# Layer 1's loop entry: ScalarE's tiles and copies placed before a norm, and GpSimd's power placed after both splits

## The chip, the cores and the metric

The kernel runs on one core of one Trainium2 chip. The metric is the device time of one execution in microseconds, the median of several runs; lower is better.

## What is computed

Four graph layers are applied one after the other to x of shape (32, 256, 128), each with a residual sum and a layer norm:

```python
x = layernorm(x + L0(x, adj))   # graph convolution with two batch norms
x = layernorm(x + L1(x, src, dst, adj))   # attention over 256 edges
x = layernorm(x + L2(x, adj))   # three matrix products with adj * adj
x = layernorm(x + L3(x, adj))   # dense graph attention
```

Layer 0 ends with a batch norm over all batches, so no batch can start layer 1 before all have finished layer 0. Layer 1 gathers the rows of its input x1 at the two ends of each edge and projects them with two matrices:

```python
Xq = H @ W_lin.T;  Xv = H @ W_val.T
e = sum(leaky_relu(Xq[src] + Xq[dst]) * a) + log(adj[src, dst] + eps)
attn = segment_softmax(e, src)
Y = segment_sum(attn * Xv[dst], src);  return Y @ W_out.T
```

The change lies where the norm after layer 0 is made and layer 1's gather and projection are done.

## The kernel before

The 32 batches are worked on in pairs. A pair is a *slot*, s = 0 or 1, and two slots make a *step* p = 0 to 7 (IT = 8); q = 2p + s counts the slots. Each engine has a program of its own, written out by hand in the order in which it works, and they meet at semaphores. Instructions on one engine run in that order: one that waits holds all behind it.

In this stage one step goes through these pieces:

- `bn_out_slot(p, s)` on ScalarE (line 1551) applies the batch norm to one slot of layer 0's output and writes the tile bnt.
- `turn_out_slot(p, s)` on TensorE (line 1963) transposes that tile into PSUM bank s.
- `sum0_slot(p, s)` on VectorE (line 875) adds it to x (tile xin, loaded by SP after an earlier sum has gone) and writes the sum to xn, which is part of keep_x.
- `variance0(p)` on VectorE (lines 190 to 203) takes mean and variance of both slots, and waits until the norm of the step before has been applied. It ends with ln_v.
- `ln_power(p)` on GpSimd (lines 209 and 212) takes the power -0.5 of ln_v, and then ln_b, mean times that power.
- `apply0(p)` on VectorE (line 905) normalizes slot 0, and `scale0(p)` on ScalarE (line 1543) slot 1. Both wait for ln_b.
- `split_x1(p, s)` on GpSimd (lines 581 and 583) splits the normalized slot into a high part (a cast) and a low part (a difference). It waits for the norm of that slot, and for the gather that used this buffer one step earlier.
- `gather_slot(p, s)` on TensorE (line 1982) multiplies the parts with the 0/1 edge matrices: 8 matmuls of 128x512 a slot, into two PSUM banks. It waits for the split and, since project uses the same banks, for both projected copies of the same slot one step earlier.
- `gathered_slot(p, s)` on ScalarE (line 1523) copies the result to SBUF; `project(p)` on TensorE (lines 1993 and 1997) projects it; `projected(p, s)` on ScalarE (lines 1533 and 1535) copies out z and vall.
- `leaky_slot` on VectorE (line 885) and `score_slot` on TensorE (line 2006, 16 matmuls of 4 columns a step) make the edge scores.

What sets the order around the change: TensorE's loop for p = 2, 3, 4 is gather(p), turn_out(p + 3), score(p - 1), project(p). ScalarE's program comes to it with edge_log and scale0(3), and then loops:

```python
scale0(3)
with act.Fori(2, IT - 3) as p:
    for s in range(2):
        bn_out_slot(p + 3, s, False)
        gathered_slot(p, s)
    scale0(p + 2)
    for s in range(2):
        projected(p, s)
```

VectorE's loop body for p is variance0(p + 2), leaky(p - 1), sum0(p + 3), apply0(p + 2). GpSimd ends its own entry with ln_power(3) and then loops over p = 3 to 6: split_x1(p, 0), ln_power(p + 1), split_x1(p, 1). `act.Fori` and `pool.Fori` are loops that the engine itself runs, with registers and a branch. After the loops steps 5 to 7 are finished without new tiles, and layers 2 and 3 follow, with layer 1's end woven into layer 2's start.

Of the kernel before, what the change touches and what calls it, by code (L numbers as in the profile page):

```python
# [34 lines left out]
IT = Q // 2  # L35
# [8 lines left out]
def build(nc, x, adj, adj_t, w1_t, w2_t, bn_cols, wv_t, wq_t, a_head, wo_t, src,  # L44
          dst, edge_cols, l2w1, l2w2, l2w3, l3w, l3a, l3w_t, out):
    ctx = ExitStack()
    with ctx:
# [11 lines left out]
        def bank(k, n=1):  # L59
            return psum[:, k:k + n, :]  # L60

        def gathered_bank(s):

            return bank(2 + 2 * s, 2)
# [86 lines left out]
        def wait_apart(eng, own, signal, value):  # L151


            if not isinstance(value, int):
                value = eng.snap(value)
            eng.wait_ge(own, 1)
            eng.wait_ge(signal, value)
# [48 lines left out]
        def ln_power(pool, p, ln):  # L206

            pool.wait_ge(ln.var, p + 1 - ln.late)
            pool.tensor_tensor(ln.r[:].rearrange("p s k -> p (s k)"), ln.v[:].rearrange("p s k -> p (s k)"), mhalf[:],  # L209
                               ALU.pow).then_inc(ln.root, 1)  # L210
            pool.wait_ge(ln.root, p + 1 - ln.late)
            pool.tensor_tensor(ln.b[:].rearrange("p s k -> p (s k)"), ln.m[:].rearrange("p s k -> p (s k)"),  # L212
                               ln.r[:].rearrange("p s k -> p (s k)"), ALU.mult).then_inc(ln.rstd, 1)
# [112 lines left out]
        def row(p):  # L326

            return lambda s, t, j: xn[:, 2 * p + s, t, j, :]
# [146 lines left out]
        def _(pool):  # L475
# [97 lines left out]
            def split_x1(p, s, first):  # L573

                q = 2 * p + s
                pool.wait_ge(ln0_done[s], q + 1)
                if not first:

                    pool.wait_ge(g_done, q - 1)
                    pool.wait_ge(x1_lo, q)  # L580
                pool.tensor_copy(x1s[0][:, s], xn[:, q]).then_inc(x1_hi, 1)
                wait_apart(pool, pz, x1_hi, q + 1)
                pool.tensor_tensor(x1s[1][:, s], xn[:, q], x1s[0][:, s], ALU.subtract).then_inc(x1_lo, 1)
# [7 lines left out]
                split_x1(2, s, False)  # L591
            ln_power(pool, 3, ln0)
            with pool.Fori(3, IT - 1) as p:
                split_x1(p, 0, False)
                ln_power(pool, p + 1, ln0)
                split_x1(p, 1, False)
            for s in range(2):
                split_x1(IT - 1, s, False)

# [838 lines left out]
        def _(act):  # L1438
# [82 lines left out]
            def gathered_slot(p, s):  # L1521
                act.wait_ge(g_done, 2 * p + s + 1)
                act.activation(g1[:, s].rearrange("p j k e -> p j (k e)"), gathered_bank(s), ACT.Copy).then_inc(g_out, 1)
# [5 lines left out]
            def projected(p, s):  # L1529
                q = 2 * p + s  # L1530

                act.wait_ge(z_done, q + 1)
                act.activation(z1[:, s, :], bank(2 + 2 * s)[:, 0, :], ACT.Copy).then_inc(z_ready, 1)
                act.wait_ge(ve_done, q + 1)
                act.activation(vall[:, :, bass.ds(2 * q, 2), :],
                               bank(3 + 2 * s)[:, 0, :].rearrange("p (t j d) -> p t j d", t=ET, j=2), ACT.Copy).then_inc(ve_out, 1)

            def scale0(p):

                act.wait_ge(ln0.rstd, p + 1 - ln0.late)  # L1540
                for k in range(4):
                    y = row(p)(1, k // 2, k % 2)
                    i = act.activation(y, y, ACT.Identity, bias=ln0.b[:, 1, k:k + 1], scale=ln0.r[:, 1, k:k + 1])  # L1543
                i.then_inc(ln0_done[1], 2)

            def bn_out_slot(p, s, first):
                q = 2 * p + s
                if not first:

                    act.wait_ge(t1_done, q - 1)  # L1550
                act.activation(bnt[:, s, :], oraw[:, q, :], ACT.Identity, bias=bco[:, 3, 2:3], scale=bco[:, 2, 2:3]).then_inc(bnt_ready, 1)
# [18 lines left out]
            def edge_log():  # L1570

                act.wait_ge(a_edge_done, 1)
                act.activation(log_a[:], bank(6)[:, 0, 0:E], ACT.Ln, bias=log_eps[:]).then_inc(log_ready, 1)
# [39 lines left out]
            for s in range(2):  # L1613
                bn_out_slot(4, s, False)
                projected(1, s)
            edge_log()
            scale0(3)
            with act.Fori(2, IT - 3) as p:
                for s in range(2):
                    bn_out_slot(p + 3, s, False)  # L1620
                    gathered_slot(p, s)
                scale0(p + 2)
                for s in range(2):
                    projected(p, s)
# [789 lines left out]
```

## Time and profile before

| | |
|---|---|
| three runs | 559.87, 561.19, 562.27 us; median 561.19 |
| span of the profiled execution | 558.5 us (first to last instruction; the page gives no other time of it) |
| TensorE busy | 533.0 us, 95% of the span |
| VectorE, ScalarE, GpSimd busy | 419.8, 371.9, 202.1 us |
| chain that ended last | TensorE 83%, VectorE 11%, ScalarE 2%, GpSimd 2% |

The span is one execution as the hardware profiler saw it; the runs are timed without it and take in what lies around the span. Times in the rows are microseconds from the first instruction. PE is TensorE, ACT ScalarE, DVE VectorE, POOL GpSimd. The granted clock is given as a share of TensorE's 2.4 GHz. Starts of matmuls are measured and their ends modelled, so neighbouring ones overlap in the rows.

### The profile page before, as it was taken

What the parts mean: (1) busy time and instruction counts of PE and PEld (TensorE: products, weight loads), DVE (VectorE), ACT (ScalarE), POOL (GpSimd) and SP (SyncE); (2) the same over time, 40 slices, a digit from 0 to 9 for tenths busy, and PEclk for the clock granted to TensorE, in tenths of its full rate; (3) what the DMA queues carried; (4) which work ended last, traced back from release to release, by engine and by line L of the source; (5) the groups of instructions that cost most, each with busy time, mean ns of one, the idle gap of its engine ahead of it and who ended that gap; (6) DMA issues with size and microseconds to landing.
All of it is one profiled execution on the core that took longest, in us unless ns stands there. A gap on an engine that the chain in (4) does not pass through costs nothing.

```text
span 558.5 us, 11129 instructions
## 1 busy us (share of the span) xinstructions
PE 533.0 (95%) x3522; PEld 467.1 (84%) x3522; DVE 419.8 (75%) x1465; ACT 371.9 (67%) x752; POOL 202.1 (36%) x245
## 2 busy tenths in 40 slices
PE   7999998988999989999999999999999999999974
PEld 6998534676888988998989999999998998989953
DVE  5899577997595643589787687788778676788797
ACT  4775793755756536355785785786688677676773
POOL 4960442254567303216127126216215214310203
PEclk9999999996999999999999999999999999999997
DMA  6621000222100000000000100100100100100002
GB/s 188 195 84 38 0 0 18 71 78 62 38 0 1 2 1 1 1 1 2 1 1 2 39 0 1 38 0 0 38 0 0 38 1 0 38 2 0 21 20 76
DMA packets 28418, 15.29 MB, mean 27 GB/s; under 512 B 2352, under 2 KB 28080, under 8 KB 28384
## 3 DMA queue, kind: packets, MB, share of 16 engines
q1 hardware_dynamic: 27536, 13.38, 8.3%
q0 software_dynamic: 560, 1.25, 0.8%
q8 instruction: 15, 0.25, 0.2%
q10 hardware_dynamic: 288, 0.26, 0.1%
q14 instruction: 19, 0.16, 0.1%
HBM read 10.69 MB, written 4.19 MB: 27 GB/s over the span
## 4 chain that ended last, share of the span: by engine, by line
PE 83%; DVE 11%; ACT 2%; issue 2%; POOL 2%; POOLq 0%; DVEq 0%; ACTq 0%
PE psum L293 15%; PE psum L295 15%; PE psum L294 15%; PE psum L2135 10%; PE psum L1934 5%; PE psum L1982 3%; PE psum L2077 3%; PE psum L2087 3%; PE psum L2006 2%; PE psum L1993 2%; PE psum L1997 2%; PE psum L2181 2%; PE psum L2163 2%; PE psum L1861 1%; DVE soft L1087 1%
## 5 line engine op out<-in xcount | busy, mean ns | idle before, releaser
L209 POOL TENSOR_TENSOR ln_r<-ln_v,mhalf 128x8 f32<-128x8 f32 x25 | 41.3, 1653 | 204.6 <-DVE ln_v L203 204.6
L2135 PE MATMUL psum<-l2w_s,h 128*128 128x128 f32 x512 | 59.7, 275 | 0.0
L2135 PEld LDWEIGHTS psum<-l2w_s,h 128*128 128x128 f32 x512 | 59.0, 192 | 0.6
L293 PE MATMUL psum<-qt_hi,l2w_s_hi 128*128 128x512 f32 x128 | 52.8, 412 | 0.0
L295 PE MATMUL psum<-qt_hi,l2w_s_lo 128*128 128x512 f32 x128 | 50.7, 396 | 0.0
L294 PE MATMUL psum<-qt_lo,l2w_s_hi 128*128 128x512 f32 x128 | 50.6, 395 | 0.0
L287 ACT ACTIVATE keep_x<-keep_x,ln_b,ln_r (+1 forms) x104 | 42.7, 487 | 2.6 <-POOL ln_b L212 2.6
L1664 ACT ACTIVATE h<-psum 128x512 f32<-128x512 f32 x60 | 34.9, 594 | 11.7 <-PE psum L295 11.6
L293 PE MATMUL psum<-wgt_hi,h_hi 128*128 128x256 f32 x128 | 37.1, 290 | 0.9 <-DVE h_lo L1064 0.9
L295 PE MATMUL psum<-wgt_hi,h_lo 128*128 128x256 f32 x128 | 35.8, 280 | 0.0
L294 PE MATMUL psum<-wgt_lo,h_hi 128*128 128x256 f32 x128 | 35.7, 279 | 0.0
L1064 DVE SCALAR_TENSOR_TENSOR h_lo<-psum,h_hi 128x1024 fp32r<-128x1024 f32 x16 | 19.6, 1225 | 18.5 <-ACT h_hi L1655 18.5
L190 DVE BATCH_NORM_STATS2 ln_st<-keep_x 128x6 f32<-128x128 f32 (+1 forms) x152 | 31.1, 277 | 1.3 <-ACT keep_x L1543 0.8
L1087 DVE SCALAR_TENSOR_TENSOR soft<-keep_x,wa 128x128 f32<-128x128 f32 x96 | 29.6, 374 | 0.0
L1934 PE MATMUL psum<-hraw,w2t 128*128 (+1 forms) x64 | 29.3, 608 | 0.0
L1075 DVE TENSOR_TENSOR s_lo<-psum,s_hi 128x512 fp32r<-128x512 f32 x16 | 11.1, 691 | 24.1 <-ACT s_hi L1668 24.1
L1660 ACT ACTIVATE qt_hi<-psum 128x1024 fp32r<-128x1024 f32 x16 | 16.4, 1024 | 19.1 <-PE psum L295 19.1
L295 PEld LDWEIGHTS psum<-qt_hi,l2w_s_lo 128*128 128x128 f32 x128 | 24.1, 188 | 5.8
L1071 DVE TENSOR_TENSOR qt_lo<-psum,qt_hi 128x1024 fp32r<-128x1024 f32 x16 | 19.5, 1221 | 11.7 <-ACT qt_hi L1660 11.7
L294 PEld LDWEIGHTS psum<-qt_lo,l2w_s_hi 128*128 128x128 f32 x128 | 24.2, 189 | 4.4
L293 PEld LDWEIGHTS psum<-qt_hi,l2w_s_hi 128*128 128x128 f32 x128 | 24.1, 189 | 4.4
L1685 ACT ACTIVATE soft<-soft,zm 128x256 f32<-128x256 f32 x56 | 27.7, 498 | 0.0
(297 smaller groups left out, 1760.7 us busy)
## 6 DMA issues: line engine op xcount, KB each, us to landing
keep_x<-in_x SPq DMA_DIRECT2D x32, 128.0 KB, 2.8
xin<-in_x SPq DMA_DIRECT2D x32, 128.0 KB, 2.2
out_x<-ob SPq DMA_DIRECT2D x24, 128.0 KB, 1.8
out_x<-keep_x SPq DMA_DIRECT2D x8, 128.0 KB, 2.0
l2w_raw<-in_l2w POOLq DMA_DIRECT2D x1, 512.0 KB, 4.9
adjs<-in_adj_t ACTq DMA_DIRECT2D x2, 128.0 KB, 2.7
adjs<-in_adj SPq DMA_DIRECT2D x2, 128.0 KB, 3.0
l2w_s<-in_l2w POOLq DMA_DIRECT2D x1, 256.0 KB, 4.8
```

What stands on the lines that cost most here:

```text
L190: i = dve.bn_stats(ln.st[:, s, k, :], y(s, k // 2, k % 2))
L209: pool.tensor_tensor(ln.r[:].rearrange("p s k -> p (s k)"), ln.v[:].rearrange("p s k -> p (s k)"), mhalf[:], ALU.pow).then_inc(ln.root, 1)
L287: i = act.activation(y(s, k // 2, k % 2), y(s, k // 2, k % 2), ACT.Identity, bias=ln.b[:, s, k:k + 1], scale=ln.r[:, s, k:k + 1])
L293: pe.matmul(o, lhs[0], rhs[0], start=start, stop=False)
L294: pe.matmul(o, lhs[0], rhs[1], start=False, stop=False)
L295: return pe.matmul(o, lhs[1], rhs[0], start=False, stop=stop)
L1064: dve.scalar_tensor_tensor(out=h1[1][:, s].rearrange("p j t f -> p (j t f)"), in0=bank(2 * s, 2).rearrange("p k c -> p (k c)"), scalar=0.0 ...
L1087: i = dve.scalar_tensor_tensor(out=soft[:, s, k, c * D:(c + 1) * D], in0=xn[:, q, k // 2, k % 2, :], scalar=1.0, in1=wa[:, c, :], op0=ALU. ...
L1664: act.activation(h2[:, s, g, :], bank(4 + g)[:, 0, :], ACT.Relu).then_inc(h2_out, 1)
L1685: i = act.activation(soft[:, s, k, :], soft[:, s, k, :], ACT.Exp, bias=zm[:, 2, s, k:k + 1], accum_out=rs[:, s, k:k + 1])
L1934: i = pe.matmul(bank(s)[:, 0, :], w2t[:, k, :], hraw[:, k, q, :], start=(k == 0), stop=(k == 1))
L2135: i = pe.matmul(bank(s)[:, 0, k * D:(k + 1) * D], h2[:, s, g, j * N + t * P:j * N + (t + 1) * P], l2w3_s[:, g, :], start=(g == 0), stop=(g ...
```

## The change

On ScalarE the tiles of step 5 and the copies of gather(2), which were the first half of the loop's first turn, are put ahead of scale0(3); the loop is written out in Python (three turns, p = 2, 3, 4), and its later turns keep their order. On GpSimd both slots are split before ln_power, in each turn of the loop. No other engine's program is touched.

```diff
@@ GpSimd
             with pool.Fori(3, IT - 1) as p:
-                split_x1(p, 0, False)
+                for s in range(2):
+                    split_x1(p, s, False)
                 ln_power(pool, p + 1, ln0)
-                split_x1(p, 1, False)
             for s in range(2):
                 split_x1(IT - 1, s, False)
@@ ScalarE
             edge_log()
+            for s in range(2):
+                bn_out_slot(5, s, False)
+                gathered_slot(2, s)
             scale0(3)
-            with act.Fori(2, IT - 3) as p:
-                for s in range(2):
-                    bn_out_slot(p + 3, s, False)
-                    gathered_slot(p, s)
+            for p in range(2, IT - 3):
+                if p > 2:
+                    for s in range(2):
+                        bn_out_slot(p + 3, s, False)
+                        gathered_slot(p, s)
                 scale0(p + 2)
                 for s in range(2):
                     projected(p, s)
```

## Rows read from the trace of the kernel before

**Rows 1.** The page: busy time of TensorE, and its clock in 40 slices.

```profile
PE 533.0 (95%) x3522; PEld 467.1 (84%) x3522; DVE 419.8 (75%) x1465; ACT 371.9 (67%) x752; POOL 202.1 (36%) x245
...
PEclk9999999996999999999999999999999999999997
```

**Rows 2.** TensorE's timeline at the entry: start, duration, work, [idle before <- releaser].

```profile
123.71 0.40 PE L1982 MATMUL psum<-sel,x1s_lo 128*128 128x512 f32 x1
127.28 1.11 PE L1963 MATMUL psum<-ident,bnt 128*128 128x128 f32 x4 [3.17 <-ACT bnt L1551]
...
129.72 3.42 PE L2006 MATMUL psum<-head_a,l 128*128 128x4 f32 x16
```

**Rows 3.** Windows, TensorE alone: stretch, length, busy, granted clock, DMA share, GB/s.

```profile
124.11:127.28 3.17, 0.01 (x1) 0.95 0.56 165
127.28:130.50 3.22, 2.79 (x13) 0.50 0.00 1
...
137.20:140.50 3.30, 3.30 (x19) 1.00 0.00 0
```

**Rows 4.** ScalarE's timeline at the entry and the loop's first turn.

```profile
120.03 0.47 ACT L1573 ACTIVATE log_a<-psum,log_eps 128x256 f32<-128x256 f32 x1
124.80 1.65 ACT L1543 ACTIVATE keep_x<-keep_x,ln_b,ln_r 128x128 f32<-128x128 f32 x4 [4.30 <-POOL ln_b L212]
...
128.66 1.01 ACT L1523 ACTIVATE g<-psum 128x1024 f32<-128x1024 f32 x1
131.59 1.65 ACT L1543 ACTIVATE keep_x<-keep_x,ln_b,ln_r  x4 [1.92 <-POOL ln_b L212]
...
139.42 0.81 ACT L1551 ACTIVATE bnt<-keep_x,bco 128x512 f32 x1
```

**Rows 5.** VectorE's timeline: ln_v of step 4, and the leaky ops at 150 us.

```profile
129.24 0.17 DVE L203 TENSOR_SCALAR ln_v<-ln_ag 128x8 f32<-128x8 f32 x1
...
150.10 1.28 DVE L885 SCALAR_TENSOR_TENSOR l<-z 128x512 f32<-128x512 f32 x2
```

**Rows 6.** GpSimd's timeline: casts of the splits, and powers.

```profile
126.25 0.61 POOL L581 CAST x1s_hi<-keep_x 128x512 fp32r x1 [1.48 <-DVE keep_x L905]
...
129.49 1.65 POOL L209 TENSOR_TENSOR ln_r<-ln_v,mhalf 128x8 f32<-128x8 f32 x1 [1.20 <-DVE ln_v L203]
...
140.81 0.61 POOL L581 CAST x1s_hi<-keep_x 128x512 fp32r x1 [7.26 <-PE psum L1982]
...
142.83 1.64 POOL L209 TENSOR_TENSOR ln_r<-ln_v,mhalf 128x8 f32<-128x8 f32 x1
...
150.71 1.15 POOL L581 CAST x1s_hi<-keep_x 128x512 fp32r x1 [3.83 <-PE psum L1982]
...
172.50 0.70 POOL L581 CAST x1s_hi<-keep_x 128x512 fp32r<-128x512 f32 x1 [0.17 <-POOL x1s_lo L583]
```

**Rows 7.** TensorE's timeline in the loop: gather(3) first and last, (4), (5), (6).

```profile
138.54 0.48 PE L1982 MATMUL psum<-sel,x1s_hi 128*128 128x512 f32 x1
...
142.12 0.39 PE L1982 MATMUL psum<-sel,x1s_lo 128*128 128x512 f32 x1
...
148.43 0.48 PE L1982 MATMUL psum<-sel,x1s_hi 128*128 128x512 f32 x1
...
158.33 0.48 PE L1982 MATMUL psum<-sel,x1s_hi 128*128 128x512 f32 x1
...
167.81 0.47 PE L1982 MATMUL psum<-sel,x1s_hi 128*128 128x512 f32 x1
```

**Rows 8.** ScalarE's timeline: scale0(7), the last of its kind.

```profile
165.06 1.65 ACT L1543 ACTIVATE keep_x<-keep_x,ln_b,ln_r 128x128 f32<-128x128 f32 x4 [1.70 <-POOL ln_b L212]
```

**Rows 9.** TensorE's timeline near the end.

```profile
542.05 0.66 PE L2286 MATMUL psum<-ident,soft 128*128 128x128 f32 x4 [2.51 <-ACT soft L1769]
```

**Rows 10.** Windows near the end, TensorE alone.

```profile
546.00:547.00 1.00, 1.00 (x7) 0.61 0.02 8
```

**Rows 11.** TensorE's timeline at the start of layer 2.

```profile
199.68 0.38 PE L293 MATMUL psum<-l2w_s_hi,pt_hi 128*128 128x256 f32 x1 [1.60 <-ACT y1t L1591]
```

## The prediction

> **What bounds the kernel now.** I read the page first: TensorE is busy 95% of the span, and its granted clock is full in every slice but the one at 126 to 140 us [rows 1]. So what delays TensorE at that place comes out at the end one for one. Then TensorE's timeline there: after the last matmul of gather(2), at 123.71, nothing starts until turn_out(5) at 127.28, 3.17 us idle, and the next score takes 3.42 us [rows 2]. The windows show why that is long: the granted clock stands at 0.50, the 1.2 GHz level, from the restart on, and is back by 137.20 [rows 3]. The release named is ScalarE's bnt tile, and ScalarE's timeline shows what stood ahead of it: idle 4.30 us, waiting for GpSimd's ln_b before scale0(3) at 124.80 [rows 4]. The tile for step 5 is queued behind a norm that TensorE doesn't need yet.
>
> In the loop that follows TensorE is the bound: gather(p) starts at 138.54, 148.43, 158.33 and 167.81, that is every 9.89, 9.90 and 9.48 us, with no idle time in between [rows 7]. But a second chain runs nearly as long. gather(p) may not write its PSUM bank before projected(p-1, slot 0) has left it, which on ScalarE stands behind scale0(p+1), which waits for GpSimd's power(p+1), which stands behind split(p, slot 0), which waits for the first half of gather(p-1). Its length: gather to split 2.28 (148.43 to 150.71), split to power 2.02 (140.81 to 142.83) [rows 6, 7]; power to scale 2.10 (129.49 to 131.59) [rows 4, 6]; scale to next gather 2.75 (165.06 to 167.81) [rows 7, 8]. Together 9.15 us: a slack of 0.3 to 0.75 a step.
>
> **The change, part by part.**
>
> *ScalarE's entry.* Step 5's two tiles and the copies of gather(2) go ahead of scale0(3). ScalarE is free at 120.50 [rows 4], so the first tile (0.81) is ready at 121.3, long before TensorE wants it. The second copy waits for gather(2)'s end, 123.71 + 0.40 = 124.11 [rows 2], takes 1.01 [rows 4], and scale0(3) starts at 125.12, 0.32 late. Behind that wait stand scale0(3) and, on VectorE, the statistics of step 4, whose ln_v moves from 129.41 to 129.73 [rows 5]. On TensorE the wait of 3.17 goes, and the half-rate work behind it: from the last matmul of a gather to the next gather is 6.31 us in the loop (142.12 to 148.43) [rows 7], so TensorE is done with project(2) at 130.0.
>
> *What is late next.* gather(3) needs projected(2, slot 0), behind scale0(4), behind power(4). On GpSimd split(3, 0) starts at 126.25 as before [rows 6], because VectorE's half of the norm isn't moved. Now split(3, 1) comes next: 126.25 + 2.02, a hand-over of 0.17 (the row at 172.50, where two splits stand together), + 2.02 = 130.46, later than ln_v, so power(4) starts there instead of at 129.49 [rows 6]. Then 2.10 and 2.75: gather(3) starts at 135.31, against 138.54. The entry gives 3.23 us, not the whole of the stall and the slow clock, and TensorE idles 5.3 us (130.0 to 135.3).
>
> *The clock after that gap.* 3.17 idle us were enough to halve it [rows 2, 3], 1.60 were not [rows 1, 11]. So I take it as halved at 135.3. How long? Near the end TensorE starts again at 542.05 and the clock is back at 546.8 (0.61 mean in that microsecond), 4.7 us [rows 9, 10]; after the gap at 124 it took 9.9 (127.28 to 137.2) [rows 2, 3]. gather(3) is one dense run of wide matmuls as the work at 542 is, while that at 127 was transposes and 4-column scores; I take 4.7, a loss of 2.35. Bounds: none, and all of gather(3) at half, 3.97.
>
> *GpSimd's order in the loop.* Power(p+1) now comes after split(p, 1) too. That puts 0.17 + 2.02 into the chain above: 9.15 + 2.19 = 11.34 us, longer than TensorE's own 9.9. This is the price of the change, and it is paid in each of the three steps, since power(5), (6) and (7) all gate a gather. GpSimd has no queue behind the power that suffers; what waits is ScalarE's scale, and behind it both projected copies, then TensorE. What split(p, 1) gains by going earlier is worth nothing: gather(p, 1) was not waiting for it. In the step behind gather(4) the cast took 1.15 beside VectorE's leaky ops (from 150.10) instead of 0.61 [rows 5, 6]; hidden now, it would be on the chain, so I add 0.54 once, with 0 and twice that as bounds. The Trainium skill (SBUF — State Buffer, "two separate sides") has GpSimd and a VectorE op with two SBUF inputs exclude each other for a whole instruction, whichever starts first. The trace agrees; by that rule the cast goes free if it starts first, and the sum below is 0.54 less.
>
> *The loop written out, and DMAs.* At its turn ScalarE's bnt starts at 139.42 with no idle time ahead [rows 4], so unrolling removes nothing to be seen: 0. No DMA is moved. SP's loads of xin wait for VectorE's sums, which move with the tiles; they were not what anything here waited for, and the steps get longer, not shorter: 0.
>
> **The sum.** gather(3) 135.31, its end 135.31 + 3.97 + 2.35 = 141.63; split(4, 1) needs that end: + 0.17 + 2.02 + 2.10 + 2.75 = gather(4) at 148.67 (before 148.43). gather(5) at + 11.34 + 0.54 = 160.55 (158.33). gather(6) at + 11.34 = 171.89 (167.81). That is 4.1 us late, and from there the order is unchanged and TensorE bound, so it stays. The gaps of about 1.5 us a step are below the 1.60 that left the clock alone. Span 558.5 + 4.1 = 562.6. The page gives no time of that execution beyond its span; the median of the runs, 561.19, stands 2.7 above it for what lies around, so 565.3.
>
> **The rivals.**
>
> *The clock hardly falls.* Three chain steps from 135.31 without loss or lock: 169.33, 1.5 late, 562.7; with the lock 563.2. For it: two gaps with a low clock are all that this trace has, and their low stretches differ by a factor of two. Against: the gap is longer than the one that did halve the clock. 0.16.
>
> *The clock stays low as long as before.* All of gather(3) at half: end 143.25, gather(4) 150.29, gather(6) 173.51, 5.7 late, 566.9. 0.12.
>
> *The other side: the entry's gain is kept.* This needs power(p+1) to stay off the chain, that is, split(p, 1) to add less than the slack of 0.75. Then the steps stay at 9.89, 9.90, 9.48 and gather(6) starts at 164.58, 3.2 early, 558.0; with the 2.35 of slow clock 0.9 early, 560.3. For it: TensorE is the bound in every loop row today. Against: a split costs 2.02 wherever it stands. 0.17, of which 0.11 for the faster end.
>
> *The change doesn't do what it says.* If TensorE's gap at 124 isn't the queue on ScalarE, gather(3) stays at 138.54 and only the longer steps are left: 5.3 late, 566.5. Against it: the transposes start 0.13 us after the bnt tile is done. 0.05.
>
> **How the numbers follow.** The forecast has 0.50. About 0.5% (2.8 us: 558.4 to 564.0) is what a measurement here can tell from no change. Faster: 0.11 from the third rival. Same: the first rival (0.16), the rest of the third (0.06) and 0.04 of the forecast's low side, 0.26. Slower: 0.46 + 0.12 + 0.05 = 0.63. The range goes from the third rival's 560.3 to the long clock with one more lock, 567.5; outside are the 0.11 below and a little above.
>
> **What would show it.** Right: turn_out(5) follows gather(2) at once; a new TensorE gap of about 5 us ahead of gather(3), released by ScalarE's vall copy; then gaps of 1 to 2 us ahead of gather(4), (5) and (6), gathers some 11.3 us apart, power(p+1) directly behind the second split with ScalarE idle 3 to 4 us for ln_b in each step. A low clock at 134 to 141 shows the second term. Wrong: gathers still 9.9 apart, or no gap ahead of gather(3).

## The result and the profile after

The changed kernel takes 567.5 us (median of seven runs, 564.01 to 569.2) against 561.19 before: ratio 1.0102, interval 1.0081 to 1.0123. It is slower by about 1%. The seven runs lie in two groups, 564.0 to 565.8 us at a mean granted clock of 0.985 or 0.986 and 567.5 to 569.2 at 0.980 or 0.981; the profiled execution is of the second, and no trace shows which low stretch the first group lacks. The profiled execution took 567.63 us, its span 565.9, 7.4 above the span before.

The page after: busy time, and TensorE's clock in 40 slices; they answer to [rows 1].

```profile
PE 534.0 (94%) x3522; PEld 467.8 (83%) x3522; DVE 416.3 (74%) x1465; ACT 370.9 (66%) x752; POOL 200.9 (36%) x245
...
PEclk9999999997998999999999999999999999999987
```

TensorE has the same work and nearly the same busy time (534.0 us against 533.0); what is new is mostly waiting. There are two places with a low clock in layer 1 instead of one. TensorE's timeline after, the first matmul of gather(3), (4), (5), (6) and (7), to be held against [rows 7]:

```profile
135.44 0.77 PE L1986 MATMUL psum<-sel,x1s_hi 128*128 128x512 f32 x1 [5.18 <-ACT vall L1535]
...
148.75 0.47 PE L1986 MATMUL psum<-sel,x1s_hi 128*128 128x512 f32 x1 [0.75 <-ACT vall L1535]
...
160.48 0.47 PE L1986 MATMUL psum<-sel,x1s_hi 128*128 128x512 f32 x1 [1.59 <-ACT vall L1535]
...
172.31 0.47 PE L1986 MATMUL psum<-sel,x1s_hi 128*128 128x512 f32 x1 [2.36 <-ACT vall L1535]
...
183.35 0.48 PE L1986 MATMUL psum<-sel,x1s_hi 128*128 128x512 f32 x1
```

Four gaps, all released by ScalarE's vall copy, stand where [rows 7] had none. gather(3) is 3.1 us earlier than before, gather(4) 0.3 later, gather(5) 2.2 later, gather(6) 4.5 later. The queue behind it, on ScalarE, shows scale0(3) to scale0(7); they answer to [rows 4, 8]:

```profile
125.05 1.64 ACT L1543 ACTIVATE keep_x<-keep_x,ln_b,ln_r 128x128 f32<-128x128 f32 x4
...
132.69 1.65 ACT L1543 ACTIVATE keep_x<-keep_x,ln_b,ln_r 128x128 f32<-128x128 f32 x4 [6.00 <-POOL ln_b L212]
...
146.00 1.65 ACT L1543 ACTIVATE keep_x<-keep_x,ln_b,ln_r 128x128 f32<-128x128 f32 x4 [3.10 <-POOL ln_b L212]
...
157.73 1.65 ACT L1543 ACTIVATE keep_x<-keep_x,ln_b,ln_r 128x128 f32<-128x128 f32 x4 [3.94 <-POOL ln_b L212]
...
169.56 1.65 ACT L1543 ACTIVATE keep_x<-keep_x,ln_b,ln_r 128x128 f32<-128x128 f32 x4 [4.05 <-POOL ln_b L212]
```

scale0(3) no longer waits; each of the others waits 3 to 6 us for GpSimd. GpSimd's timeline after shows why; it answers to [rows 6] (casts of the turn p = 5, its power, the cast and the power of p = 6):

```profile
151.02 0.83 POOL L581 CAST x1s_hi<-keep_x 128x512 fp32r x1 [5.06 <-PE psum L1986]
...
153.79 0.61 POOL L581 CAST x1s_hi<-keep_x 128x512 fp32r x1 [0.25 <-POOL x1s_lo L583]
...
155.78 1.64 POOL L209 TENSOR_TENSOR ln_r<-ln_v,mhalf 128x8 f32<-128x8 f32 x1
...
162.75 0.61 POOL L581 CAST x1s_hi<-keep_x 128x512 fp32r x1 [5.06 <-PE psum L1986]
...
167.23 2.02 POOL L209 TENSOR_TENSOR ln_r<-ln_v,mhalf 128x8 f32<-128x8 f32 x1
```

The power starts 4.5 to 4.8 us after the first cast, where [rows 6] had 2.0 (140.81 to 142.83), and that with GpSimd idle 5 us before the cast: the engine isn't short of time, its order is wrong for the one who waits. The granted clock after, in windows with TensorE alone (stretch, length, busy, clock, DMA share, GB/s), answers to [rows 3]:

```profile
133.00:134.00 1.00, 0.00 (x0) 0.98 0.71 185
134.00:135.00 1.00, 0.00 (x0) 0.50 0.72 195
...
140.00:141.00 1.00, 1.00 (x5) 0.60 0.00 0
178.00:179.00 1.00, 1.00 (x3) 0.67 0.00 0
181.00:182.00 1.00, 1.00 (x5) 0.62 0.00 0
```

The slow clock after the old stall (127 to 137) is gone. There are two others: 134.0 to 140.8, over the gap and most of gather(3), and 178.3 to 181.8, over the first half of project(6). The latter makes gather(6) to gather(7) 11.04 us instead of 9.38, 1.66 more.

The 7.4 us of the span are therefore 4.5 at gather(6), 1.66 behind it, and the rest near the end: the transposes of [rows 9] start at 548.66 after, 6.6 late (0.45 of it picked up somewhere in 365 us), and from there to the end it is 17.24 us against 16.45, because the clock was already halved when they started.

```profile
548.66 1.11 PE L2290 MATMUL psum<-ident,soft 128*128 128x128 f32 x4 [2.52 <-ACT soft L1773]
```

They took 0.66 before. That last 0.8 goes with neither part of the change: of the kernels below, GpSimd's part alone has 0.66 there and so has the kernel with both fillers, while ScalarE's part alone and the kernel with one turn have 1.12. Each of these is one execution, so no edit can be made answerable for it.

### The profile page after: what moved, and what is told of

Read it like the earlier page. It is cut to its first block, busy times and chain, and to the rows that moved or that the text cites. A ratio compares the mean times of both kernels' runs of the same rounds, so it can differ in the third digit from the quotient of the medians.

```text
span 565.9 us, 11089 instructions
## 1 busy us (share of the span) xinstructions
PE 534.0 (94%) x3522; PEld 467.8 (83%) x3522; DVE 416.3 (74%) x1465; ACT 370.9 (66%) x752; POOL 200.9 (36%) x245
## 4 chain that ended last, share of the span: by engine, by line
PE 81%; DVE 9%; POOL 4%; ACT 4%; issue 1%; POOLq 0%; DVEq 0%
PE psum L293 15%; PE psum L295 15%; PE psum L294 15%; PE psum L2139 9%; PE psum L1938 5%; PE psum L1986 4%; PE psum L2081 3%; PE psum L2091 3%; PE psum L2185 2%; PE psum L2167 2%; PE psum L1865 1%; ACT keep_x L1543 1%; POOL x1s_lo L583 1%; POOL ln_r L209 1%; PE psum L2010 1%
## 5 line engine op out<-in xcount | busy, mean ns | idle before, releaser
L1668 ACT ACTIVATE h<-psum 128x512 f32<-128x512 f32 x60 | 34.8, 594 | 11.7 <-PE psum L295 11.6
L1986 PE MATMUL psum<-sel,x1s_hi 128*128 128x512 f32 x64 | 27.6, 432 | 11.1 <-ACT vall L1535 9.9
L1071 DVE TENSOR_TENSOR qt_lo<-psum,qt_hi 128x1024 fp32r<-128x1024 f32 x16 | 19.6, 1222 | 11.7 <-ACT qt_hi L1664 11.7
```

The source lines that it names most:

```text
L1668: act.activation(h2[:, s, g, :], bank(4 + g)[:, 0, :], ACT.Relu).then_inc(h2_out, 1)
L1986: i = pe.matmul(gathered_bank(s)[:, j, :], x1s[h][:, s, t, j, :], sel[:, t].rearrange("p k e -> p (k e)"), start=(n == 0), stop=(n == 3))
```

## The experiments

Nine kernels were run; each is compared with runs of the kernel before on the same chip.

### The two parts apart

ScalarE's part alone is the change without its GpSimd hunk. GpSimd's part alone:

```diff
             with pool.Fori(3, IT - 1) as p:
-                split_x1(p, 0, False)
+                for s in range(2):
+                    split_x1(p, s, False)
                 ln_power(pool, p + 1, ln0)
-                split_x1(p, 1, False)
```

Expected of ScalarE's part:

> The change's ScalarE part alone, GpSimd in its old order. Chain theory (the cost is GpSimd's second split ahead of the power, which gates each gather): power(4) starts at ln_v, about 129.8, so gather(3) starts near 134.6 instead of 135.4, after a TensorE gap of 4 to 5 us that still halves the clock for some microseconds; after it the gathers are 9.9 to 10 us apart again with no gap, gather(6) is 1 to 4 us ahead of the kernel before (167.81), and the time is 557 to 560.5 us. Rival (ScalarE's new queue order or its written-out loop costs the time): slower than before, near 565 to 567, with gaps ahead of gather(4) to gather(6) as in the changed kernel.

Expected of GpSimd's part:

> The change's GpSimd part alone, ScalarE as before. Chain theory: the stall at 124 and its slow clock stay, gather(3) stays near 138.5, and then the gathers are 11.3 to 11.9 us apart with TensorE gaps of 1 to 2.4 us released by ScalarE's vall copy; gather(6) near 173.1, time 566 to 568.5 us. Rival (the loss is the slow clock after the new 5 us gap, which this kernel does not have): gathers 9.9 us apart, time within 1 us of before.

Measured: ScalarE's part alone 558.79 us against 560.78, ratio 0.9962 (0.9943 to 0.9981), a gain of 0.4%. GpSimd's part alone 567.86 against the same, 1.0125 (1.0098 to 1.0152). TensorE's timeline, gather(3) to (6), first of ScalarE's part, then of GpSimd's:

```profile
134.52 0.76 PE L1986 MATMUL psum<-sel,x1s_hi 128*128 128x512 f32 x1 [3.83 <-ACT vall L1535]
...
147.19 0.48 PE L1986 MATMUL psum<-sel,x1s_hi 128*128 128x512 f32 x1
...
157.08 0.48 PE L1986 MATMUL psum<-sel,x1s_hi 128*128 128x512 f32 x1
...
166.53 0.47 PE L1986 MATMUL psum<-sel,x1s_hi 128*128 128x512 f32 x1
```

```profile
138.83 0.48 PE L1982 MATMUL psum<-sel,x1s_hi 128*128 128x512 f32 x1
...
150.24 0.47 PE L1982 MATMUL psum<-sel,x1s_hi 128*128 128x512 f32 x1 [1.26 <-ACT vall L1535]
...
162.08 0.47 PE L1982 MATMUL psum<-sel,x1s_hi 128*128 128x512 f32 x1 [1.72 <-ACT vall L1535]
...
173.91 0.47 PE L1982 MATMUL psum<-sel,x1s_hi 128*128 128x512 f32 x1 [2.35 <-ACT vall L1535]
```

With GpSimd's old order the gathers behind gather(4) are 9.89 and 9.45 apart and there is no gap after the first (gather(3) itself runs at the low clock, from 133.8 to 140.6); with its new order alone they are 11.41, 11.84 and 11.83 apart, though this kernel has the old stall and no 5 us gap behind it. Its gather(6) came at 173.91, 0.8 later than expected. The loss belongs to GpSimd's order; ScalarE's written-out loop costs nothing that shows.

### One turn only

The turn p = 4 alone splits both slots before the power; the other turns keep the order.

```diff
+            split_x1(3, 0, False)
+            ln_power(pool, 4, ln0)
+            split_x1(3, 1, False)
+            for s in range(2):
+                split_x1(4, s, False)
+            ln_power(pool, 5, ln0)
-            with pool.Fori(3, IT - 1) as p:
+            with pool.Fori(5, IT - 1) as p:
```

> The kernel before, with GpSimd's new order in one turn only (p = 4, so power(5) comes behind both splits and gates gather(4)). Chain theory: gather(3) to gather(4) takes 11.3 us instead of 9.89, the next two stay at 9.90 and 9.48, the time is 1.4 us above before. Rival (one turn's slack absorbs it): 9.9 in all three.

```profile
138.47 0.48 PE L1988 MATMUL psum<-sel,x1s_hi 128*128 128x512 f32 x1
...
149.75 0.47 PE L1988 MATMUL psum<-sel,x1s_hi 128*128 128x512 f32 x1 [1.12 <-ACT vall L1541]
...
159.64 0.48 PE L1988 MATMUL psum<-sel,x1s_hi 128*128 128x512 f32 x1
...
169.15 0.47 PE L1988 MATMUL psum<-sel,x1s_hi 128*128 128x512 f32 x1
```

TensorE's timeline again: 11.28, then 9.89 and 9.51. One turn costs its 1.4 us once and nothing else moves. The one timed run, 561.77 against 560.78, is 1.0 above, which alone would prove little.

### The slow clock

Useless matmuls fill the gaps; they write a bank that nobody reads at that time. The first filler, ahead of gather(3):

```diff
-            with pe.Fori(2, IT - 3) as p:
+            gather(2, False)
+            turn_out(5, False)
+            score(1)
+            project(2)
+            pe.wait_ge(log_ready, 1)
+            spin(10, 6)
+            with pe.Fori(3, IT - 3) as p:
```

> The changed kernel, with 10 useless 128x256 matmuls (about 4.7 us) put into TensorE's gap ahead of gather(3). They replace no work and write a bank that nobody reads. If the slow clock of gather(3) is a term of its own: clock 1.00 from 124 to 150, gather(3) lasts 3.97 us instead of 6.4, gather(4) starts near 146.8 instead of 148.75, and the gathers behind it stay 11.3 to 11.9 apart; the time falls by about 2 us against the changed kernel. If all of the loss were the clock: the gathers come back to 9.9 apart and the time to that before or below.

The second, ahead of gather(6):

```diff
             project(IT - 3)
+            pe.wait_ge(sm, 2)
+            spin(4, 6)
             gather(IT - 2, False)
```

> The changed kernel with 4 useless 128x256 matmuls (about 1.9 us) in the last of the new gaps, the 2.36 us ahead of gather(6); they replace no work and write a bank that nobody reads. If that gap is what lets the clock fall behind it (in the changed kernel at 178.3, well after TensorE had started again): clock 1.00 from 150 to 200, gather(6) unmoved near 172.3, gather(7) 9.4 us behind it at 181.7 instead of 183.35. If the 4-column scores at 176 to 178 make the fall by themselves: the slow stretch stays, and gather(7) with it.

And both:

> The changed kernel with both fillers (10 matmuls ahead of gather(3), 4 ahead of gather(6)). What is then left of the loss is the longer chain alone: clock 1.00 from 124 to 200, gather(3) to (6) 11.3 to 12 us apart, gather(7) 9.4 behind gather(6), near 180.3; so about 3.2 us above the kernel before, 564 us (563 to 565.5), and 2.5 to 3.5 us below the changed kernel. If the fillers only moved the waiting, the time stays near 567.

TensorE's timeline with both, gather(3) to (7):

```profile
135.00 0.47 PE L1986 MATMUL psum<-sel,x1s_hi 128*128 128x512 f32 x1 [0.89 <-ACT vall L1535]
...
147.00 0.47 PE L1986 MATMUL psum<-sel,x1s_hi 128*128 128x512 f32 x1 [1.85 <-ACT vall L1535]
...
158.73 0.47 PE L1986 MATMUL psum<-sel,x1s_hi 128*128 128x512 f32 x1 [1.59 <-ACT vall L1535]
...
170.58 0.47 PE L1986 MATMUL psum<-sel,x1s_hi 128*128 128x512 f32 x1 [0.63 <-ACT vall L1535]
...
179.95 0.48 PE L1986 MATMUL psum<-sel,x1s_hi 128*128 128x512 f32 x1
```

Both fillers give 563.7 us against 560.86, ratio 1.0058 (1.0037 to 1.008): what the longer chain costs alone, net of the entry's gain. The clock is 1.00 from 124 to 200, and gather(6) to (7) is 9.37. The gathers stay 11.7 to 12.0 apart, so the chain remains. Against the 1.0102 of the changed kernel, the low clock in layer 1 is some 2.5 us of the loss, an estimate from the two ratios. The first filler alone made gather(3) to (4) 11.99 (136.02 to 148.01) instead of 13.31; that is 1.3 us for the slow clock, not the 1.9 expected, since the chain there is some 0.6 longer than forecast: with gather(3) at full clock the cast of split(4, 0) meets VectorE's leaky ops and takes 1.08 us instead of 0.61, and the difference behind it 1.53 instead of 1.27. Its one time is 566.88, so the 2 us expected of it don't show: it kept a slow stretch ahead of and in gather(6), 171.2 to 174.6, and one near the end. The second alone (564.81 in one run) took the stretch at 178 away; the windows of that kernel:

```profile
175.00:180.00 5.00, 5.00 (x35) 1.00 0.00 0
180.00:185.00 5.00, 5.00 (x30) 1.00 0.00 0
```

gather(6) starts at 172.19 there and gather(7) at 181.57, as forecast. The three profiled kernels with this gap of 2.35 or 2.36 us open (the changed one, GpSimd's part alone, the first filler alone) all show a low stretch there, the two with it filled show none: it takes the gap, and the scores by themselves don't do it.

### The scale taken off TensorE's path

Here GpSimd keeps the new order, and ScalarE's projected copies, with the next tiles behind them, go ahead of the scale in the turns p = 2, 3, 4; the turn p = 5 stays as it was:

```diff
             for p in range(2, IT - 3):
                 if p > 2:
-                    for s in range(2):
-                        bn_out_slot(p + 3, s, False)
-                        gathered_slot(p, s)
-                scale0(p + 2)
+                    gathered(p)
                 for s in range(2):
                     projected(p, s)
+                for s in range(2):
+                    if p + 4 < IT:
+                        bn_out_slot(p + 4, s, False)
+                scale0(p + 2)
```

> The changed kernel, GpSimd's new order kept, with ScalarE's projected copies of a step (and the next tiles) put ahead of scale0(p + 2) in the turns p = 2, 3, 4, so that the scale, and the power behind it, no longer gate gather(3), (4) and (5). Chain theory (GpSimd's order costs only because the scale stands ahead of the projected copies): no gap ahead of gather(3), which starts near 130.0; no gap released by the vall copy ahead of gather(4) and (5); gather(6), whose turn keeps the old order, still about 11.3 us after gather(5). A new wait is likely ahead of score(2), because VectorE makes leaky(2) behind the statistics that wait for scale0(4): some 3.5 us. Time about 558.5 (556 to 561). Rival (GpSimd's second split costs by itself, by its time on the engine or by what it shares with VectorE): the gathers stay 11.3 to 11.9 us apart and the time near that of the changed kernel.

It took 568.82 us in one run, and the forecast of its time was far off, though gather(3) did start at 130.34 and no vall copy released gather(4) or (5). TensorE's timeline shows the new wait, ahead of score(2) and score(3), and the old one ahead of gather(6):

```profile
139.62 2.95 PE L2011 MATMUL psum<-head_a,l 128*128 128x4 f32 x16 [4.44 <-DVE l L885]
...
155.97 2.29 PE L2011 MATMUL psum<-head_a,l 128*128 128x4 f32 x16 [2.86 <-DVE l L885]
...
176.26 0.47 PE L1987 MATMUL psum<-sel,x1s_hi 128*128 128x512 f32 x1 [2.18 <-ACT vall L1535]
```

The last line is a control within the same execution: only gather(6) has the scale ahead of its copies, and only there the wait for vall stays. I had seen the first of the new waits, but took it for a single one of 3.5 us. It closes a ring instead: project(3) stands behind score(2), scale0(5) on ScalarE behind project(3)'s copies, VectorE's statistics behind the scale, leaky(3) behind the statistics, score(3) behind leaky(3); and the clock stood at half behind both waits (140.3 to 147.2 and 157.4 to 164.2). So the next kernel also moves leaky on VectorE, and treats the turn p = 5 in the same way (shown is VectorE's loop body; the leaky behind that loop goes too, and ScalarE's scale in turn p = 5 goes behind the copies):

```diff
                 variance0(p + 2, False)
-                if behind:
-                    leaky(p - 1)
                 sum0(p + 3)
+                leaky(p)
                 apply0(p + 2)
```

> As the one before, and in the turn p = 5 too, and with VectorE's leaky(p) taken after sum0(p + 3) instead of behind the next step's statistics. Chain theory: gathers near 130.0, 139.9, 149.8 and 159.3, TensorE without a gap and at clock 1.00 from 124 to 180, about 8.5 us below the kernel before: 552.3 (550.5 to 555). Rival (GpSimd's second split costs by itself): gathers 11.3 apart, 557 or more.

And the same with GpSimd's old order:

> As the one before with GpSimd in the old order (power between the two splits). Chain theory: with the power off TensorE's path the new order is the better one: here split(3, 1) comes behind power(4) and is done near 134, so the second half of gather(3) waits 2 us for it (released by GpSimd's x1s_lo), and later steps are 9.9 apart: 2 to 3 us above the one before, 553.5 to 556. Rival (the old order is better in itself): below the one before.

The first takes 553.16 us against 560.66, ratio 0.9868 (0.9834 to 0.9901), the fastest kernel of this study. Its timeline, gather(3) to (6):

```profile
130.68 0.48 PE L1985 MATMUL psum<-sel,x1s_hi 128*128 128x512 f32 x1
...
140.58 0.48 PE L1985 MATMUL psum<-sel,x1s_hi 128*128 128x512 f32 x1
...
150.47 0.48 PE L1985 MATMUL psum<-sel,x1s_hi 128*128 128x512 f32 x1
...
159.72 0.48 PE L1985 MATMUL psum<-sel,x1s_hi 128*128 128x512 f32 x1
```

From 124 to 165 us there is no gap and no slow clock, with 9.9 us a step and 9.25 in the last, and GpSimd's new order in place. With the old order it is 556.43 us, 0.9922 (0.9899 to 0.9946), just above the range expected. TensorE's timeline of that kernel, the second half of gather(3) and then gather(4):

```profile
134.72 0.50 PE L1985 MATMUL psum<-sel,x1s_hi 128*128 128x512 f32 x1 [2.05 <-POOL x1s_lo L583]
...
144.34 0.47 PE L1985 MATMUL psum<-sel,x1s_hi 128*128 128x512 f32 x1
```

The wait of 2.05 us is the one forecast, and the clock stood at half behind it, from 135.2 to 138.6; gather(4) is 3.8 us later than in the kernel before this one. So GpSimd's order isn't bad in itself. With the scale ahead of the copies the power is urgent and the second split is not; with the scale behind them it is the other way round, and the same change of order gains 3.3 us (556.43 to 553.16; the two intervals just touch, and the rows carry the difference).

## Why the prediction was right, and what it missed

The direction, the mechanism and its place were right, and the measured time lies in the range, on its upper end: 567.5, forecast 565.3. In spans the miss is larger, 565.9 against 562.6: of the 2.7 us that the forecast added for what lies around the span the runs show only 1.73 (567.63 against 565.9), so by that estimate the profiled execution before was 1 us faster than its median. The 3.3 us are 0.4 at gather(6), 1.66 of low clock behind it, and the 0.45 and 0.8 further on.

- *ScalarE's entry.* Forecast: scale0(3) at 125.12, TensorE's stall gone. Measured 125.05, and turn_out(5) follows gather(2).
- *What is late next.* Forecast: gather(3) at 135.31 after a gap of 5.3; measured 135.44 after 5.18. Power(4) started at 130.73, not 130.46, for another reason than forecast: VectorE's ln_m took 1.17 us instead of 0.17 while GpSimd's split ran, and ln_v was late.
- *The slow clock after that gap.* Forecast: half for 4.7 us from the restart, a loss of 2.35; measured 5.4 (135.44 to 140.8), and gather(3) took 6.24 us to the next transposes (135.44 to 141.68) instead of 3.81, 2.43 more. The fillers show it as a term of its own. But the size came out by luck, since 4.7 is a misreading: windows of the kernel before show full clock for the first 1.3 us after the restart at 542.05, so the low stretch there was 3.4 us (543.4 to 546.8) and would have given a loss of 1.7. The last slice of the page, a 7 in [rows 1], is a second one below full clock, which the first paragraph of the prediction passes over:

```profile
542.00:543.00 1.00, 0.95 (x6) 1.00 0.00 0
543.00:544.00 1.00, 1.00 (x5) 0.68 0.00 0
```

The rival that had all of gather(3) at half gave 566.9, nearer to the measured time, but also by luck: gather(3) lost 2.43 us, not 3.97.
- *The longer chain.* Forecast: gather(4), (5), (6) at 148.67, 160.55, 171.89; measured 148.75, 160.48, 172.31. The two parts apart, the single turn and the order of copies and scale show its three links: GpSimd's order, a price for each turn, and the scale ahead of the copies. The rival that kept the entry's gain falls with the same runs; it would have needed that second split to hide.
- *VectorE beside GpSimd.* I added 0.54 once. The turn at 151.02 took 4.76 us from cast to power where 4.21 were reckoned without it, 0.55 more. The turn at 162.75 had 0.27 (4.48), and its power took 2.02 us instead of 1.64 beside VectorE's scans, which the forecast left out.
- *The step that failed* is the sentence that gaps of about 1.5 us a step are below the 1.60 that left the clock alone. Its own sum gives more: 1.98 us ahead of gather(5) (11.88 - 9.90) and 1.86 ahead of gather(6) (11.34 - 9.48). And [rows 9] have a gap of 2.51 us, with the fall of the clock just shown behind it, so between 1.60 and 2.51 nothing was known. The gaps were 0.75, 1.59 and 2.36. The last was longer than the sum's because GpSimd's split and power were slower beside VectorE (0.27 and 0.38); that step, without new tiles, has only 9.48 us of TensorE work. The clock fell behind it and cost 1.66 us in the profiled execution. With that the forecast would have been 567.0.
- *The written-out loop and DMAs*, costed at nothing: ScalarE's part alone is faster than before, so no cost is hidden there.

## What to carry to other kernels

An order on a helper engine is right or wrong only against what stands ahead of the urgent result in the *next* engine's queue; write the ring of waits down, with durations, and compare its length with the busiest engine's step. If an engine is the bound by half a microsecond a step, two microseconds put into the ring beside it come out in every step, less that half. And before a helper is put in another order, look whether what it feeds must stand ahead of the urgent work at all: with ScalarE's entry, the scale behind the copies and leaky moved together the kernel came to 553.16 us, where ScalarE's entry with GpSimd's old order came to 558.79.

## What the runs showed of the hardware

- A TensorE gap shorter than the 3.17 us of the old stall was often enough for a halved clock, and not always in the gap. Of five gaps of 2.05 to 2.36 us four had a low stretch of some 3.4 us beside them. It began at 178.3 in the changed kernel, 6 us after the restart and with TensorE busy again (dense matmuls, then 4-column scores); at 175.2 in GpSimd's part alone, 1.3 after the restart; at 135.2 in the last kernel above, 0.5 after it; at 171.2, within the gap, with the first filler. The fifth, 2.18 us ahead of gather(6) in the first kernel with the scale off the path (176.26), had none. Gaps of 1.59, 1.72 and 1.85 had none either. So the length of such a gap alone did not decide it; each is one execution.
- The gap of 2.51 or 2.52 us near the end stands in all eleven traces, and each has a low stretch there. It began between 1.7 us before the restart (547.0 in the changed kernel) and 1.4 after it (543.4 in the kernel before), and lasted some 3.4 or 6.8 us.
- VectorE and GpSimd hold each other up even for tiny work: ln_m, 8 columns and one input, took 1.17 us instead of 0.17 beside a GpSimd difference, and GpSimd's power on 8 columns 2.02 instead of 1.64 beside VectorE's scans. The Trainium skill (SBUF — State Buffer, "two separate sides") has GpSimd and a VectorE operation that takes the port pair they share, by two SBUF inputs or by a two-port mode, wait for the whole of the other's instruction. The trace agrees for ln_m, which ended with the difference (129.41 + 1.17 = 130.58 against 129.28 + 1.26 = 130.54); that a two-port mode is the reason there, no run shows. The rows are VectorE's and GpSimd's of the changed kernel:

```profile
129.41 1.17 DVE L201 TENSOR_SCALAR ln_m<-ln_ag 128x8 f32<-128x8 f32 x1
...
129.28 1.26 POOL L583 TENSOR_TENSOR x1s_lo<-keep_x,x1s_hi 128x512 fp32r<-128x512 f32 x1
```

The kernel before had the same at 161.50, ln_m in 1.18 us beside GpSimd's difference at 161.37.
